# The start of the state-space stage in a six-block kernel, rebuilt by halves of the tokens

## The reference, cut to what matters

```python
proj = layernorm(x) @ in_proj_w.T                 # gate 8192, xBC 10240, dt 128
gate, xBC, dt = split(proj)
xBC = silu(causal_conv4(xBC) + conv_b)            # x 8192; B and C, 8 groups of 128
dt = clip(softplus(dt + dt_bias), 0.001, 100)     # per token and head, 128 heads
dA = dt * A                                       # A = -(1..128)
cs = cumsum(dA) within chunks of 128 tokens
L[l, s] = exp(cs[l] - cs[s]) for s <= l
Y = (C B^T * L) (x dt)                            # in a chunk
states = B^T (exp(cs[end] - cs) * x dt)           # carried into the next chunk
Y += exp(cs) * (C prev_state);  Y += x * D
out = groupnorm(Y * silu(gate)) @ out_proj_w.T
```

## Time and profile before

| | |
|---|---|
| time, 3 runs | 2317.57 us median (2316.78 to 2317.88) |
| the profiled execution | 2317.2 us, of it the span of instructions 2315.4 us |
| PE (TensorE) busy | 94% of the span |
| DVE (VectorE), ACT (ScalarE), POOL (GpSimd) busy | 74%, 61%, 45% |
| granted TensorE clock, mean | 0.972 of full speed |
| last down product issued before the state-space block | 573.77 us |
| first `y_products` (step 0) | 652.25 us |

### The profile page before, as it was taken

The page is one execution under the profiler, slowest core; times in us unless marked ns, Lnnn a source line. Parts: engine busy times, 40 slices in busy tenths (PEclk is TensorE's granted clock), DMA queues, the critical chain, the costliest instruction groups (busy, mean ns, idle before and its releaser), DMA issues. The chain is left out here.

```text
span 2315.4 us, 34456 instructions
## 1 busy us (share of the span) xinstructions
PE 2169.9 (94%) x12539; PEld 1761.2 (76%) x12554; DVE 1704.7 (74%) x2688; ACT 1409.7 (61%) x3050; POOL 1045.6 (45%) x758
## 2 busy tenths in 40 slices
PE   6879978999599999999999999999999999996999
PEld 6756667888488887887887887887887888775887
DVE  7767767232388889889889889888988988985221
ACT  3267743332577766876767767776877677762332
POOL 4366544443135445435533634444445443554442
PEclk9899999999799999999999999999999999997999
DMA  3000010332223323232323323323332332221332
GB/s 128 1 1 1 1 42 28 95 92 73 105 70 141 114 82 127 99 113 83 137 92 110 105 95 111 119 83 114 109 115 83 137 119 83 89 104 32 91 96 82
DMA packets 62519, 202.50 MB, mean 87 GB/s; under 512 B 6928, under 2 KB 6928, under 8 KB 53904
## 3 DMA queue, kind: packets, MB, share of 16 engines
q1 hardware_dynamic: 62352, 200.31, 25.4%
HBM read 197.39 MB, written 2.88 MB: 86 GB/s over the span
## 5 line engine op out<-in xcount | busy, mean ns | idle before, releaser
L480 POOL TENSOR_TENSOR wAl<-rawA,wAh 128x512 fp32r<-128x512 f32 x233 | 325.6, 1412 | 421.4 <-ACT wAh L595 421.0
L1389 PE MATMUL ps<-xTh,wAh 128*128 128x512 f32 x1512 | 429.0, 406 | 22.4 <-DVE work L1211 14.0
L1389 PE MATMUL ps<-xTl,wAh 128*128 128x512 f32 x1512 | 417.1, 398 | 0.0
L1389 PE MATMUL ps<-xTh,wAl 128*128 128x512 f32 x1512 | 414.3, 396 | 0.0
L1211 DVE SCALAR_TENSOR_TENSOR work<-ps,chp,work 128x510 f32<-128x510 f32 (+2 forms) x480 | 354.2, 744 | 55.0 <-ACT work L771 44.7
L1389 PEld LDWEIGHTS ps<-xTh,wAh 128*128 128x128 f32 x1512 | 277.8, 190 | 94.8 <-DVE work L1211 15.1
L1389 PEld LDWEIGHTS ps<-xTl,wAh 128*128 128x128 f32 x1512 | 286.8, 190 | 69.4
L1389 PEld LDWEIGHTS ps<-xTh,wAl 128*128 128x128 f32 x1512 | 284.9, 188 | 69.2
L805 ACT ACTIVATE eb<-eb,gc 128x128 f32<-128x128 f32 x1024 | 312.3, 390 | 14.9 <-DMA eb<-scr_decays 14.9
L486 POOL TENSOR_TENSOR wBl<-rawB,wBh 128x512 fp32r<-128x512 f32 x108 | 142.6, 1333 | 387.6 <-ACT wBh L599 387.6
L532 POOL TENSOR_TENSOR sqt<-gt 128x512 f32<-128x512 f32 x112 | 154.8, 1382 | 120.1 <-DVE gt L1266 112.0
(11 more groups left out here) (183 smaller groups left out, 3957.2 us busy)
## 6 DMA issues: line engine op xcount, KB each, us to landing
eb<-scr_decays SPq DMA_DIRECT2D x64, 1536.0 KB, 6.4
rawA<-ma_in SPq DMA_DIRECT2D x144, 256.0 KB, 3.7
rawA<-fa_in SPq DMA_DIRECT2D x88, 256.0 KB, 2.6
rawB<-mb_in SPq DMA_DIRECT2D x64, 256.0 KB, 2.8
rawB<-fb_in SPq DMA_DIRECT2D x44, 256.0 KB, 2.6
x<-x_in SPq DMA_DIRECT2D x8, 256.0 KB, 6.3
x_out<-x SPq DMA_DIRECT2D x8, 256.0 KB, 2.7
wqraw<-wqkv_in SPq DMA_DIRECT2D x1, 1536.0 KB, 10.3
```

The lines of the kernel that those rows point to most:

```text
L480: nc.gpsimd.tensor_tensor(wAl[:, slot, :], rawA[:, slot, :], wAh[:, slot, :].bitcast(F32), ALU.subtract).then_inc(A_lo, 1)
L1389: return nc.tensor.matmul(o, l, r, start=start, stop=end, **kw)
```

## The change

The prologue is rebuilt so that each half of the tokens (512 columns, tiles 0 to 3 and 4 to 7) goes through it by itself.

- TensorE: chunk 0 goes ahead of SwiGLU's last down product. The even chunks 2, 4 and 6, which need only the first half of the tokens, go between the transposes of tiles 4 to 7. The time-step product, its transposes, the running sums and their transposes are done for each half, with chunks 1, 3, 5 and 7 between them.
- ScalarE: the four time-step operations, `csf` and `ctok` are done by halves (512 columns each), in a new order among the convolutions. `erow` comes last, after `decay_exp` of both halves. `spans` of the very first pair reads `ctok` itself.
- VectorE: SwiGLU's last four additions are taken between the statistics of tiles 4 to 7, behind the taps of chunk 0.
- DMA: the running sums are written to the scratch by halves and pair 0's rows are read by halves, in three DMAs each (`first_rows`). The rows of the states are computed from the sums of a chunk's end by an exponential in place (`first_exp`). `erow` is written when it is there, and pair 1's rows follow it.
- Memory: the first five convolutions have buffers of their own (`sq`, `sqt`, `gt[:, 1]`), only the sixth uses `work`; `dts` lies over `yTh`, no longer over `eb`.
- SyncE's queue: weight tile 5 is loaded after the first half's rows, tiles 6 and 7 before the second half's.

The diff, cut to its core:

```diff
+    FIRST = [0, 2, 4, 6, 1, 3, 5, 7]
+    FIRST_BANK = {0: 0, 2: 2, 4: 1, 6: 3, 1: 0, 3: 2, 5: 1, 7: 0}
+    def conv_acc(g, c):
+        n = conv_index(g, c)
+        if n == 0 or n == 1:
+            return sq[:, 512 * n:512 * n + 512]
+        if n == 2:
+            return sqt[:, :]
+        if n == 3 or n == 4:
+            return gt[:, 1, 512 * (n - 3):512 * (n - 3) + 512]
+        return work[:, n % 2, :]
@@ SyncE
-        for i in range(6):
+        for i in range(5):
             mamba_A(i, 0)
         mamba_B(0, 0)
         mamba_B(1, 0)
-        sp.wait_ge(m_csf, 2)
-        sp.dma_start(scr[:, 0:NT, :], csf[:, :, :]).then_inc(m_scr, 16)
+        def first_rows(p):
+            rows, last = slice(4 * p, 4 * p + 4), slice(4 * p + 1, 4 * p + 4, 2)
+            sp.wait_ge(m_csf, p + 1)
+            sp.dma_start(scr[:, rows, :], csf[:, rows, :]).then_inc(m_scr, 16)
+            sp.wait_ge(m_scr, 16 * (p + 1))
+            sp.dma_start(eb[:, 0, :, rows, :], scr[0:2, rows, :].partition_broadcast(P)).then_inc(m_first[p], 16)
+            for h in range(2):
+                sp.dma_start(eb[:, 0, h, NT + 2 * p:NT + 2 * p + 2, :],
+                             scr[h, last, :].partition_broadcast(P)).then_inc(m_first[p], 16)
+        first_rows(0)
+        mamba_A(5, 0)
+        for i in step_tiles(0, False):
+            mamba_A(i, 0)
+        first_rows(1)
+        mamba_B(2, 0)
+        mamba_B(3, 0)
         sp.wait_ge(m_erow, 1)
         sp.dma_start(scr[:, NT:NT + B, :], erow[:, :, :]).then_inc(m_scr, 16)
-        sp.wait_ge(m_scr, 32)
-        mamba_rows(0, 0)
-        step(0, 0)
+        sp.wait_ge(m_scr, 48)
+        mamba_rows(1, 0)
@@ GpSimd
         swiglu(0, 3, 0, 0)
+        lo_A(A0M + 4)
+        lo_A(A0M + 5)
         for t in range(AHEAD, NT):
             layer_rstd(4, t)
-        for n in range(4, 6):
-            lo_A(A0M + n)
@@ ScalarE
         fetch_params(1, 0)
         conv_start(0, 0, 1)
+        hi_A(A0M + 4)
+        hi_A(A0M + 5)
+        layer_hi(4, 4, 4)
+        dt_act(0, 0)
+        dt_act(0, 1)
+        layer_hi(4, 5, 5)
+        dt_act(0, 2)
+        conv_start(0, 2, 1)
+        layer_hi(4, 6, 4)
+        layer_hi(4, 7, 5)
+        dt_act(0, 3)
+        conv_start(0, 4, 1)
+        hi_B(B0G)
+        hi_B(B0G + 1)
+        dt_tokens(0)
+        dt_act(1, 0)
+        dt_act(1, 1)
+        dt_act(1, 2)
+        running_sums(0)
+        dt_act(1, 3)
+        conv_start(0, 1, 1)
+        conv_start(0, 3, 1)
+        dt_tokens(1)
+        token_sums(0)
+        conv_silu(0, 0)
+        conv_silu(0, 2)
+        conv_start(0, 5, 1)
+        running_sums(1)
+        conv_silu(0, 4)
+        conv_silu(0, 1)
+        conv_silu(0, 3)
+        gate_silu(0, 6)
+        token_sums(1)
+        spans(0, 0, 0)
+        conv_silu(0, 5)
+        gate_silu(0, 7)
+        hi_A(A0G + 5)
+        end_decay(0)
+        end_decay(1)
+        first_exp(0)
+        spans(0, 0, 1)
+        first_exp(1)
         act.wait_ge(m_csf, 2)
         nc.scalar.activation(erow[:, :, :], csf[:, 1:NT:2, :], ACT.Exp).then_inc(m_erow, 1)
         step(0, 0, first=True)
@@ VectorE
         swiglu(0, 3)
+        taps(0, 0)
+        dve.wait_ge(m_out, DN[0] + 2 * NF)
+        add_down(4)
+        layer_stats(4, 4)
+        ...
+        layer_lo(4, 7, 5)
+        dt_clip(0)
+        taps(0, 2)
+        decay_rate(0)
+        taps(0, 4)
+        dt_clip(1)
+        taps(0, 1)
+        decay_rate(1)
+        taps(0, 3)
+        taps(0, 5)
         for b in range(B):
             mask_cb(0, b)
+        end_weights(0)
+        end_weights(1)
         scale_x(0, 0, 0)
         scale_x(0, 0, 1)
+        decay_off(0, 0, 0)
         decay(0, 0, 0)
+        decay_off(0, 0, 1)
         decay(0, 0, 1)
@@ TensorE
+                if s == 2 * NF and i == 0:
+                    chunk(0, 0)
         swiglu(0, 3, 0, 0)
+        dt_product(0)
+        chunk(0, 2)
+        layer_transpose(4, 4, 4, False)
+        chunk(0, 4)
+        layer_transpose(4, 5, 5, False)
+        chunk(0, 6)
+        layer_transpose(4, 6, 4, False)
+        layer_transpose(4, 7, 5, False)
+        dt_product(1)
+        dt_transpose(0)
+        chunk(0, 1)
+        sums(0)
+        chunk(0, 3)
+        sums_transpose(0)
+        dt_transpose(1)
+        chunk(0, 5)
+        sums(1)
+        chunk(0, 7)
+        sums_transpose(1)
+        pe.wait_ge(m_gate, 1)
         for b in range(B):
             bc(0, b)
+        pe.wait_ge(m_u, 2)
         transposes(0, 0, 0)
         transposes(0, 0, 1)
         step(0, 0, first=True)
```

More of the change, by code:

```diff
@@ L227, in build @@
     m_sqt = sem("m_square")
+    m_first = [sem(f"m_first_rows_loaded{i}") for i in range(2)]
     m_neg = sem("m_decay_exponent")
@@ L721, in _ @@
         act.wait_ge(l0_lora, 2 * NT)
+        act.wait_ge(chp_s, 16)
         swiglu(0, 3, 0, 0)
[L723 to L739, removed]
         def fetch_params(slot, g):
@@ L1348, in step, with add_down @@
                 mean_square(g, 5)
-        taps(0, 0)
-        taps(0, 1)
[L1352 to L1359, removed]
+        def add_down(t):
+            nc.vector.scalar_tensor_tensor(out=x[:, t, :], in0=ps[:, t, :], scalar=0.5, in1=x[:, t, :],
+                                           op0=ALU.mult, op1=ALU.add).then_inc(x_new, 1)
@@ L1610, in in_chunk @@
             n = A0G + tile
[L1611 to L1614 removed]
+            pe.wait_ge(A_lo, g * NA_G + n + 1)
+            if g == 0 and c < 8:
+                bank = chunk_bank(g, c)
+                if c == 0:
+                    pe.wait_ge(f_h, 2 * NF - 1)
+                elif c == 2:
+                    pe.wait_ge(f_g, 2 * NF)
+                elif c == 6:
+                    pe.wait_ge(m_dts, 1)
+                elif c % 2:
+                    pe.wait_ge(ln_lo, 40)
+                    pe.wait_ge(m_tap, 3 * {1: 0, 3: 1, 5: 2, 7: 3}[c] + 3)
+            else:
                 p = c - 3
@@ L1767, in _ @@
-        mm(ps[:, 3, :].rearrange("p (b h) -> p b h", b=B), low, dA[:, 0:NT:2, :], True, True).then_inc(m_end, 1)
-        chunk(0, 4)
-        for a in range(2):
-            pe.wait_ge(m_csf, a + 1)
-            pe.wait_ge(m_dttok, a + 1)
-            for t in range(4):
-                last = nc.tensor.transpose(ps[:, 6 + a, t * P:(t + 1) * P], csf[:, 4 * a + t, :], ident)
-            last.then_inc(m_ctt, 1)
-        for c in range(5, 8):
-            chunk(0, c)
-        pe.wait_ge(m_ctok, 2)
@@ L1778, in _, with dt_product, dt_transpose @@
-        pe.wait_ge(m_u, 1)
+        def dt_product(p):
+            wh, wl = wA(A0M)
+            cols = slice(512 * p, 512 * p + 512)
+            product(ps[:, (3, 6)[p], :], wh, wl, [xTh[:, kc, cols] for kc in range(KC)],
+                    [xTl[:, kc, cols] for kc in range(KC)]).then_inc(m_dtp, 1)
+        def dt_transpose(p):
+            pe.wait_ge(m_dtd, p + 1)
+            for t in range(4):
+                cols = slice((4 * p + t) * P, (4 * p + t + 1) * P)
+                last = nc.tensor.transpose(ps[:, (7, 6)[p], t * P:(t + 1) * P], dts[:, 0, cols], ident)
+            last.then_inc(m_dtt, 1)
@@ new lines, in sums, with sums_transpose @@
+        def sums(p):
+            pe.wait_ge(m_dA, p + 1)
+            if p:
+                pe.wait_ge(m_csf, 1)
+            for t in range(4):
+                last = mm(ps[:, 4, t * P:(t + 1) * P], dA[:, 4 * p + t, :], tri, True, True)
+            last.then_inc(m_cst, 1)
+            if p:
+                pe.wait_ge(m_dttok, 2)
+            mm(ps[:, YBANK[p], 0:2 * P].rearrange("p (b h) -> p b h", b=2), low, dA[:, 4 * p:4 * p + 4:2, :],
+               True, True).then_inc(m_end, 1)
+        def sums_transpose(p):
+            pe.wait_ge(m_csf, p + 1)
+            if p:
+                pe.wait_ge(m_ctok, 1)
+            else:
+                pe.wait_ge(m_dttok, 1)
+            for t in range(4):
+                last = nc.tensor.transpose(ps[:, 7, t * P:(t + 1) * P], csf[:, 4 * p + t, :], ident)
+            last.then_inc(m_ctt, 1)
```

209 lines of the change are left out of this document (111 added, 98 removed).

## The result

The changed kernel took 2300.42 us (median of 4 runs, 2297.53 to 2300.66) against 2317.18 for the kernel before beside it (2316.42 to 2317.88). The ratio is 0.9925, with a 95% interval of 0.9908 to 0.9942. The prediction was 2300.0. A second set of five runs gave 2297.88 against 2316.98, 0.9921 (0.9908 to 0.9935). The profiled execution has a span of 2298.7 us against 2315.4: 16.7 us less.

The account below looks back on a forecast made before the run. The prologue was taken as bound by a chain through all engines, the rest by TensorE. The first output product coming 17.6 us earlier (658.9 against 676.55) gave 2317.6 - 17.6 = 2300.0 us, range 2295 to 2307.

Parts of the forecast that it names:

- Step 1: Prologue until the second time-step product: TensorE paces it, and that product starts at 591.7 us, 4.1 later than before.
- Step 2: ScalarE's queue from 591.7 us to erow at 623.8: ScalarE is the bound for 32 us with under 1 us of waits.
- Step 3: Halved rows of pair 0 land before their spans want them, so the 6.0 us wait goes.
- Step 4: Pair 1's rows, behind erow, land at 632.5 us: ScalarE waits 6.8 us, TensorE stands from 632.3 to 640.7.
- Step 5: Pair 1's spans to full TensorE: first product of step 1 at 649.15, first output product at 658.9, 17.6 us earlier.
- The sum: Whole kernel: 17.6 us less than before, 2317.6 to 2300.0 us.
- Whatever the prologue gives TensorE earlier, the rest keeps: Behind 655 us TensorE never stands still, so the prologue's whole gain of 17.6 us stays in the total.
- the group boundaries: TensorE's 1.93 us stalls: half clock behind one costs about 0.9 us, at six of seven; widens every case some 2 us.
- Later rows: Rival: pair 1's rows take 10.8 us to land, 4.2 later, gain 13.4, time 2304.2; chance 0.13.
- The shorter wait: Rival: the wait for pair 1's rows isn't there; 6.1 us more by the ledger, only part possible, 2297; chance 0.15.
- The rival of a dear switch: Rival: each of ScalarE's seven table loads costs twice its 1.28 us, 9.0 us in all, time 2309.0; chance 0.03.
- The slower case: Rival: pair 1's rows need 29 us to land, making the kernel slower by 5 us, 2322; chance 0.03.

Follow-up runs that it names:

- e4: Changed kernel with a one-column Exp and a one-column Silu added ahead of pair 0's spans (two table switches more): 2302.10 us.
- e2: Changed kernel with the running sums written whole, behind both halves, and pair 0's rows read after that: 2302.54 us.
- e1: Changed kernel with the exponential erow moved ahead of the two end decays in ScalarE's queue: 2291.04 us.
- e5: Changed kernel with 22 unused matmuls of 512 columns added behind chunk 11 of step (0,0), where TensorE stands still: 2297.32 us.
- e10: Changed kernel with 7 unused matmuls ahead of the last output-product token tile, in step 2 of each group but the first: 2298.86 us.
- e11: Changed kernel with erow ahead of the end decays and the same 7 unused matmuls as e10: 2291.42 us.
- e3: Kernel before, with silus, a weight part, convolution starts and gates moved ahead in ScalarE's queue around pair 0's spans and exponentials: 2302.55 us.
- e6: e1 with chunk 8 also moved ahead of the transposes of pair 0's x: 2294.26 us.

## Why the prediction was right, point by point

**Step 1** held in its time: the second time-step product at 591.86 (591.7 forecast). That TensorE paces the stretch holds only in part, since TensorE waited 1.67 us for VectorE's remainder ahead of that product.

**Step 2** held: csf of half 0 ended at 599.67 (599.4), the transposes of pair 0 began at 617.44 (617.5), `erow` ended at 623.16 (623.8). ScalarE had 29.84 busy of 32 us; its waits were 2.0 us (0.84, 0.53 and 0.61), not under 1, but the marks behind them came within 0.7 us of the forecast. e4 shows that what is added to its queue is added to the end. The price of a table load was the row's 1.28 us.

**Step 3** held: no wait for pair 0's rows, and without the halved write 5.0 us of it (e2).

**Step 4** held: a wait of 7.01 us for pair 1's rows (6.8), its spans at 631.94 (632.5), and e1 gives it back. TensorE's stall was 5.67 us, not 8.4, because it ended 0.8 us sooner and TensorE came 1.9 us later to it: TensorE stood at half clock behind the 3.56 us stall at 617 (2.06 us for four matmuls, not 1.10), and the first `y_products` began at 625.62, not 624.0. My ledger had half clock only behind the longer stall.

**Step 5** gave the right time in part by errors that cancel, which is luck. The first product of step 1 came at 649.10 (649.15 forecast), but not because `decay` set it: VectorE's two decays ran from 645.86 on, and the first ended at 647.07, 2.1 us sooner than in my ledger. TensorE was late by its half clock, which I had taken as 3.3 us long and hidden. It was 5.5 us long (the clock is 0.50 from 639.9 to 645.4, and 0.15 x 18.40 / 0.5 from the fourth stretch above gives the same) and not hidden; e5 puts 0.9 us on it. The two small waits on the way to the output products, 0.5 us in the ledger, weren't there: TensorE was busy for 18.40 of 18.40 us, and from the first product of step 1 to the first output product it took 9.26 us in both kernels.

**The sum** was 17.6. P gave 18.5: 0.5 of the difference are those two waits, and 0.3 is that the changed kernel reached P later than the kernel before. S took back 1.5, so that 16.7 are left in the profiled execution and 16.8 between the medians. "Whatever the prologue gives TensorE earlier, the rest keeps" thus holds but for these 1.5 us, and the prediction had named their largest part: it is the seventh fall of the clock (seven against six), 0.9 us, in the note on the group boundaries. Another 0.3 is the wait for taps, and 0.3 is unexplained. The same two terms account for most of the spread of S: with 0.93 us a fall and the wait for taps taken off, the ten profiles without added matmuls in S lie within 1.0 us (1395.7 to 1396.6) instead of 3.7. With the seven fillings of e10 and e11 it is 1397.6 and 1398.1. The prediction's 2 us for S was about the right width and half of the reason; it didn't have the late rows in S.

**The rivals.** Later rows (10.8 us to land) didn't occur; from issue to spans it was 6.7 us. The shorter wait didn't either. By the ledger's own figures no landing could have removed it, since the rows leave at 625.9 and their spans are reached at 625.7; issuing them sooner did (e1), and its 7.1 us are more than the 6.1 given there, by the clock. The rival of a dear switch is refuted by e4. The slower case had no trace of itself.

## What to carry to other kernels

In a hand-ordered queue the question isn't only what an instruction waits for, but who stands behind it: four lines moved in one queue (e3) gave two thirds of what a rebuilt stage gave. When a wait is taken away, look for the next consumer of the same resource: here pair 0's rows were made early, and pair 1's, behind an `erow` moved to the end, took the wait over, at 7.1 us for a single line. Compare prologues by events inside the trace, since the totals of nearly identical code up to them differed by 3 us. And when an engine's lost time is given back and the total doesn't move, look for the wait that took it before calling the loss free: the half clock in S cost 0.9 us a group, and e10 lost as much to late rows and to its own added matmuls.

## What the runs showed of the hardware that wasn't expected

A TensorE stall of 3.56 us (at 617.4) was followed by half clock, as was the 5.67 us one. Stalls of 1.93 us in a stage that is otherwise full were followed by half clock in some groups and not in others (the mean clock of the earlier trace rows: 1.00 and 0.58), and with 7 matmuls in them in none. Where nothing else stood in the way, a group with such a fall took 184.3 us and one without 183.3 to 183.4. S was hardly shorter at full clock (e10) than with seven falls, because other waits took the time. The DMA of 1536 KB that spreads two heads' rows took from issue to the start of its spans 6.5 us in e1, 6.7 in the changed kernel and 7.7 in e6, and the 256 KB write ahead of it 2.0 us, but 2.6 in e4. Within S the same DMA, in the same place of the same kernel, landed 6.6 us behind its issue in one profiled execution and 7.8 in another, and TensorE waited 1.0 us only in the second.
